# A fused transformer kernel: the third layernorm applied behind the mix, and logits made from the transposed second residual

## The reference, cut to what matters

```python
x = x + relu_attention(layernorm(x), ctx)          # q, k, v with relu, scores over 128 keys
x = x + quantised_ffn(layernorm(x))                # FP6 blocks of 32, one 512x512 weight
# third block: W is 512 x 1024, b has 512
n = layernorm(x)
x = x + n @ W[:, :512].T + (mean(ctx) @ W[:, 512:].T)[:, None, :] + b
# fourth block
n = layernorm(x)
logits = n @ Wg + bg                               # 16 experts
probs = softmax(logits, axis=-2)                   # over the 2048 rows of a batch
vals, idx = top_k(probs transposed, 128)           # 128 rows for each expert
h = relu(n[idx] @ w1 + b1); h = relu(h @ w2 + b2); h = h @ w3 + b3
x = x.at[idx].add(h * vals)
```

## Time and profile before

| what | value |
|---|---|
| runs (3) | 833.03, 833.72, 834.87 us; median 833.72 |
| profiled execution, its own time | 834.25 us |
| its span | 832.4 us, mean granted clock 0.953 |
| PE busy | 727.7 us (87%) |
| DVE busy | 591.7 us (71%) |
| POOL busy | 451.6 us (54%) |
| ACT busy | 412.1 us (50%) |
| DMA | 103.53 MB, 53787 packets |

### The profile page before, as it was taken

How to read it: one execution, slowest core, us unless ns; L and a number is a source line. 1 busy time by engine, 2 the same in 40 slices (tenths; PEclk the granted TensorE clock), 3 DMA queues, 4 the chain that set the end, 5 groups by cost and what they waited for, 6 DMA issues and landing times.

```text
span 832.4 us, 12007 instructions
## 1 busy us (share of the span) xinstructions
PE 727.7 (87%) x4202; PEld 623.9 (75%) x4202; DVE 591.7 (71%) x1010; ACT 412.1 (50%) x564; POOL 451.6 (54%) x627
## 2 busy tenths in 40 slices
PE   1967899999999999999999400899999999999994
PEld 1755788787878878787777300799999999999993
DVE  4685789798897979778695498466666766666751
ACT  4553445555554646445333220366666566666540
POOL 3537788788787878768675060314333344333231
PEclk9979899999999999999999855899999999999998
DMA  9600022121221212111111314448887787887642
GB/s 299 237 0 14 25 76 77 53 89 64 84 70 68 74 53 89 66 39 52 39 65 53 122 69 158 128 134 238 233 244 236 211 251 236 236 240 246 179 88 37
DMA packets 53787, 103.53 MB, mean 124 GB/s; under 512 B 5216, under 2 KB 5984, under 8 KB 53728
## 3 DMA queue, kind: packets, MB, share of 16 engines
q1 hardware_dynamic: 46560, 85.99, 30.9%
q0 software_dynamic: 7168, 16.78, 8.9%
HBM read 77.20 MB, written 25.17 MB: 123 GB/s over the span
## 4 chain that ended last, share of the span: by engine, by line
PE 80%; DVE 10%; POOL 3%; DMA 2%; issue 2%; ACT 2%; SPq 0%; ACTq 0%; POOLq 0%; DVEq 0%
PE bank L238 70%; PE bank L245 8%; DVE pack L1151 1%; PE bank L444 1%; DVE left L1158 1%; DVE pos L1153 1%; DMA x<-x 1%; ACT xn L700 1%; DVE bn L936 1%; POOL rstd L1308 0%; PE bank L555 0%; POOL rstd L1307 0%; DVE x L1088 0%; DMA tok<-xn,ids 0%; DVE s L981 0%
## 5 line engine op out<-in xcount | busy, mean ns | idle before, releaser
L1406 POOL DMA_INDIRECT out<-y,ids x32 | 76.2, 2382 | 173.8 <-DVE y L1271 169.3
L948 DVE TENSOR_TENSOR w_l<-w_raw,w_h 128x2048 fp32r<-128x2048 f32 x45 | 103.0, 2289 | 31.3 <-ACT w_h L704 30.2
L700 ACT ACTIVATE xn<-x,rstd 128x512 f32<-128x512 f32 x96 | 78.6, 819 | 80.0 <-POOL rstd L1312 79.9
L899 ACT ACTIVATE h<-bank,b 128x512 f32<-128x512 f32 x64 | 44.0, 687 | 107.7 <-PE bank L238 107.7
L936 DVE BATCH_NORM_STATS2 bn<-x 128x6 f32<-128x512 f32 x128 | 88.2, 689 | 9.6 <-DMA x<-x 6.3
L704 ACT ACTIVATE w_h<-w_raw 128x2048 fp32r<-128x2048 f32 x48 | 90.6, 1924 | 4.6 <-DMA w_raw<-w 4.6
L948 DVE TENSOR_TENSOR hT_l<-h,hT_h 128x512 fp32r<-128x512 f32 x64 | 44.2, 691 | 67.2 <-ACT hT_h L905 67.2
L245 PE MATMUL bank<-ident,xn 128*128 128x128 f32 x384 | 60.4, 281 | 24.7 <-ACT xn L700 21.4
L245 PEld LDWEIGHTS bank<-ident,xn 128*128 128x128 f32 x384 | 48.5, 145 | 40.6 <-ACT xn L700 28.8
L1308 POOL TENSOR_TENSOR rstd<-rstd,minus_half 128x1 f32<-128x1 f32 x128 | 73.1, 571 | 10.7
L1307 POOL TENSOR_SCALAR rstd<-mean_var 128x1 f32<-128x1 f32 x128 | 31.6, 247 | 82.6 <-DVE mean_var L941 76.0
(11 more groups left out here) (200 smaller groups left out, 2189.5 us busy)
## 6 DMA issues: line engine op xcount, KB each, us to landing
w_raw<-w SPq DMA_DIRECT2D x48, 1024.0 KB, 6.9
x<-x SPq DMA_DIRECT2D x32, 256.0 KB, 2.7
out<-x SPq DMA_DIRECT2D x32, 256.0 KB, 2.0
xn<-xn SPq DMA_DIRECT2D x32, 256.0 KB, 2.0
mask<-mask_t SPq DMA_DIRECT2D x8, 256.0 KB, 3.0
stage<-wc_t SPq DMA_DIRECT2D x2, 1024.0 KB, 8.5
stage<-wq SPq DMA_DIRECT2D x1, 1024.0 KB, 8.2
stage<-wk SPq DMA_DIRECT2D x1, 1024.0 KB, 11.4
```

The source lines that it names most:

```text
L700: act.activation(dst[:, :], src[:, :], ACT.Identity, bias=r[:, n, 2:3], scale=r[:, n, 1:2])\
L899: act.activation(h32[n % 2][:, :], ps_hid[n % 4][:, :], ACT.Relu, bias=bias)
L948: dve.tensor_tensor(dst, src, hi_part, ALU.subtract).then_inc(sem, 1)
L1406: pool.indirect_dma_start(out=out_rows, out_offset=bass.IndirectOffsetOnAxis(ap=ids[:, r:r + 1], axis=0), in_=y[e % 2][b][:, :], in_offset ...
```

## The change

The third layernorm is no longer applied to `x2` before it is transposed. With r = 1/sqrt(var + eps) and m the mean of a row of `x2`, the product is `((x2 - m) r) @ Wc = r (x2 @ Wc')`, where Wc' is Wc with the mean of each of its columns taken off. So `x2` itself is transposed (`x2T_h`, `x2T_l`), and `x3 = r (x2 @ Wc') + x2 + bias` is one operation of VectorE. `xn3` and its ScalarE operation are gone, and `rstd_of(2)` has two operations.

The logits are linear in `x3` up to the fourth layernorm's own factor r4, so they are made from `x2T` with weights of the setup: for each row `x2 @ Wg'` (Wg' is Wg with its column means off) and `x2 @ Gm`, with Gm the mean-free product of Wc' and Wg'. `seg = r4 (x2 @ Wg' + c + r3 (x2 @ Gm)) + bg`. `xn4` is no longer transposed: `t4`, `x4T_h` and `x4T_l` are gone. `logits(g)` is now 8 matmuls, four with 64 columns of weights over the high part and four with 32 over the rest, and stands one step earlier (5, 9, ..., 33). The four 16-row parts go to `seg4` by four DMAs; r3 and r4 of every tile are stored as rows in DRAM, loaded broadcast over partitions after phase 1, and VectorE combines all in six operations ahead of top-k.

New products of the setup, all in plain float32: `mix_means` (4 matmuls with 512 columns of rows moved) and `gate_means` (4 with 16) before `t1(8)`; `mix_gate` (16 with 16) at the end of step 0, from W in its natural layout, loaded once more over 1 MB; `mix_gate_means` (4 with 16) at the end of step 1; `bias_gate` (4 with 2) at the end of step 2. The six warming matmuls of step 34 are gone, and so are the nine that stood there for `t4`.

```diff
     def logits_of(k):
-        g = (k - 6) // GRP
-        return g if (k - 6) % GRP == 0 and 0 <= g < G else None
+        g = (k - 5) // GRP
+        return g if (k - 5) % GRP == 0 and 0 <= g < G else None
...
@sync, after the setup's loads
+        sp.wait_ge(sm.a_set, A["wc1"])
+        sp.wait_ge(sm.g_set, GS["wc1"])
+        sp.dma_start(stage[0][:, :, :], chunked(io.wc[:, 0:D])).then_inc(sm.c_wcn, 16)
+        sp.wait_ge(sm.d_set, V["all"])
+        sp.dma_start(io.cb.rearrange("(a b) n -> a b n", a=1), cbias[0:1, :, :]).then_inc(sm.c_cg, 16)
+        sp.wait_ge(sm.c_cg, 16)
+        for b in range(B):
+            sp.dma_start(cbcol[:, b, :], io.cb[b].rearrange("(c p) -> p c", p=P),
+                         allow_slow_non_contiguous=True).then_inc(sm.c_cg, 16)
...
@sync, after phase 1
+        for i in (1, 0):
+            for b in range(B):
+                rows = io.r[i].rearrange("(b a s t) -> b a s t", b=B, a=1, t=GT)[b].to_broadcast([E, GB, GT])
+                sp.dma_start(rseg[i][64 * b:64 * b + 64, :], rows).then_inc(sem_rseg[i], 16)
...
@tensor
-        def t4(j):
...
         def t3(j):
-            pe.wait_ge(sm.a_xn3, j + 1)
...
+            pe.wait_ge(sm.d_x2, j + 1)
...
-            four_transposes(pe, ps_ta, xn3).then_inc(sm.p_t3, 1)
+            four_transposes(pe, ps_ta, x2[j % 2]).then_inc(sm.p_t3, 1)
...
         def logits(g):
...
+            pe.matmul(ps_s[0:4 * E, :], wgs[:, 0, :], x2_h[:, 0, :], start=True, stop=False)
+            for d in range(C):
+                pe.matmul(ps_s[0:2 * E, :], wgs[:, d, 0:2 * E], x2_l[:, d, :], start=False, stop=False)
+            for d in range(1, C):
+                last = pe.matmul(ps_s[0:4 * E, :], wgs[:, d, :], x2_h[:, d, :], start=False, stop=(d == C - 1))
...
+        def column_means(bank, parts):
+            for d in range(C):
+                last = pe.matmul(bank, mean_w[:, :], parts(d), start=(d == 0), stop=(d == C - 1))
...
+        def mix_gate():
+            pe.wait_ge(sm.c_wcn, 16)
+            pe.wait_ge(sm.a_s, 1)
+            for c in range(C):
+                for o in range(C):
+                    last = pe.matmul(ps_s[:, c * E:(c + 1) * E], stage[0][:, o, c * P:(c + 1) * P], wgf[:, o, 0:E],
+                                     start=(o == 0), stop=(o == C - 1))
...
         q_chunk(*q_of(4))
+        mix_means()
+        gate_means()
         t1(8)
...
-            if valid(k - 3):
-                if not q_units(k):
-                    pe.wait_ge(sm.a_q, N)
-                    keep_warm(4 if valid(k) else 9, wq_h, ps_q[0])
-                t4(k - 3)
+            if valid(k - 3) and k < LAST - 1 and not q_units(k):
+                pe.wait_ge(sm.a_q, N)
+                keep_warm(4 if valid(k) else 9, wq_h, ps_q[0])
...
+            if k == 0:
+                mix_gate()
+            if k == 1:
+                mix_gate_means()
+            if k == 2:
+                bias_gate()
...
@scalar: wc_h now waits for VectorE's subtraction and stands behind norm1(9); in step 2
+            if k == 2:
+                act.wait_ge(sm.p_cb, 3)
+                act.activation(cg[:, :], ps_s[0:E, 128:128 + B], ACT.Copy).then_inc(sm.a_cb, 1)
...
@vector: the subtraction of the column means in the setup, and in phase 1
+            if what == "wc1c":
+                dve.wait_ge(sm.p_set, T["wc1m"])
+                mean = ps_c[:, :].unsqueeze(1).to_broadcast([P, C, D])
+                lo(sm.d_set, stage[0][:, :, :], stage[0][:, :, :], mean)
...
-                dve.tensor_tensor(x3[j % 2][:, :], ps_c[:, :], x2[j % 2][:, :], ALU.add).then_inc(sm.d_x3, 1)
+                dve.scalar_tensor_tensor(x3[j % 2][:, :], ps_c[:, :], r_all[0][:, j:j + 1], x2[j % 2][:, :],
+                                         ALU.mult, ALU.add).then_inc(sm.d_x3, 1)
...
+            if k == 0:
+                dve.wait_ge(sm.p_cb, 1)
+                dve.tensor_copy(wgf[:, :, E:2 * E], ps_s[:, 0:C * E].rearrange("p (c e) -> p c e", c=C))\
+                    .then_inc(sm.d_wg, 1)
+            if k == 1:
+                dve.wait_ge(sm.p_cb, 2)
+                mean = ps_s[:, 0:E].unsqueeze(1).to_broadcast([P, C, E])
+                lo(sm.d_wg, wgf[:, :, E:2 * E], wgf[:, :, E:2 * E], mean)
...
@gpsimd: wc_l stands behind the rest of the queries of unit 4; its subtraction waits for wc_h as before
```

More of the change, by code:

```diff
@@ L102, in build @@
     bk = place("bk", [P, C])
-    bg = place("bg", [E, 1])
+    bg_seg = place("bg_seg", [P, 1])
+    c_seg = place("c_seg", [P, 1])
+    cg = place("logit_shift", [E, B])
+    cbcol = place("mix_bias_col", [P, B, C])
+    r_all = [place(f"rstd_all{i}", [P, N]) for i in range(2)]
     eps_exp = place("minus_half", [P, 1])
@@ L140, in build @@
     at_lt = top[0]
[L141 removed]
+    lt = place("lt", [4 * E, GT])
     q8 = place("q8", [P, D], FP8)
@@ L527, in keys, with mix_gate_means, bias_gate @@
+        def mix_gate_means():
+            pe.wait_ge(sm.d_wg, 1)
+            column_means(ps_s[:, 0:E], lambda d: wgf[:, d, E:2 * E]).then_inc(sm.p_cb, 1)
+        def bias_gate():
+            pe.wait_ge(sm.c_cg, 16 * (1 + B))
+            pe.wait_ge(sm.d_wg, 2)
+            for c in range(C):
+                last = pe.matmul(ps_s[0:E, 128:128 + B], wgf[:, c, 0:E], cbcol[:, :, c], start=(c == 0), stop=(c == C - 1))
+            last.then_inc(sm.p_cb, 1)
         def keys():
```

188 lines of the change are left out of this document (114 added, 74 removed).

## The result

| | before | changed |
|---|---|---|
| runs of this comparison | 833.03 to 834.97 us, median 834.3 (4) | 844.78 to 847.26 us, median 846.07 (4) |
| ratio | 1 | 1.0143, 95% interval 1.0118 to 1.0167 |
| profiled execution, its span | 834.25, 832.4 us | 847.26, 845.4 us |
| PE, DVE, POOL, ACT busy | 727.7, 591.7, 451.6, 412.1 us | 717.3, 585.3, 449.8, 372.1 us |
| DMA packets | 53787 | 65997 |

The kernel is slower by 1.4%. The forecast of 832.9 us, and its whole range up to 840, are missed. Every engine is busy for less time than before, as the prediction worked out, and the time went up all the same. So most of the loss lies in waiting.

The account below looks back on a forecast made before the run. TensorE's instruction sum was taken to bound steps 4 to 26, a loop through several engines steps 28 to 31, then VectorE's top-k. +15.9 - 15.7 - 1.6 + 0.7 and 0.1 less for `wg` made -0.8, so 832.9 us; range 827 to 840.

Parts of the forecast that it names:

- Removed from TensorE: Steps 4 to 26: dropping `t4` and a third of the logits' matmuls shortens TensorE's bound stretch by 15.7 us.
- GpSimd keeps up: Steps 4 to 26: GpSimd needs 10.1 us a step against TensorE's 10.27, tight, so it does not become the bound.
- Steps 28 to 31: Loop through several engines: the step with logits falls from 11.20 to 9.83 us, two others by 0.13 each; -1.6 us.
- Added to the start: Setup and first steps, counted to `t2(3)`: the new products, loads and waits cost +15.9 us.
- (c): Start: SP, held by `wc_l` and loads, brings tile 10 at 94.3, so `ffn(0)` starts at 96.2 instead of 83.76, +12.4 us.
- My lower end: Start: the lower bound of 2.7 us for tile 10's landing, with 7.9 as upper bound and 4.9 taken.
- (b): Start: GpSimd's `wc_l` begins at 77.7, the first rstd after it is 5.2 us later, `t2(0)` at 86.4, `mix_gate` until 92.4.
- The rival with four times a transposition's cost: Start: the small float32 products cost 0.44 us each at full clock, `mix_gate` lasts 7.0 us, total 836.7 us; chance 0.21.
- a load by single elements: Start: `mix_bias_col` is 1024 one-element descriptors, unpriced, speaking for the upper side of tile 10's 2.7 to 7.9 us.
- (d): Steps 1 and 2: half clock, new products and the wait for `bias_gate` before `xdT_h` put `t2(3)` at 130.8.
- The tail: From `t2(31)` to top-k's first maximum: 31.6 us instead of 30.9, the shorter logits' chain spent on a serial step; +0.7 us.
- it lands after 1.9 us: Tail: the last of four logits' pieces, issued at 23.1 us after `t2(31)`, lands 1.9 us later, at 25.0.

Follow-up runs that it names:

- e7: Changed kernel with `mix_gate` and `bias_gate` moved into step 1, the means into step 2, their waits off the path of `xdT_h` and `xdT_l`: 843.87 us.
- e5: Changed kernel with GpSimd writing `x2 + bias` into x3's buffer, so it waits for an earlier store of x3 instead of `t3`: 846.92 us.
- e2: Changed kernel without the 8 row stores of tiles 28 to 31, broadcast loads reading x instead (logits' scaling wrong): 837.95 us.
- e3: Changed kernel with the logits' pieces issued ahead of x3, its normalisation and the rstd row of the same step: 847.53 us.
- e10: Changed kernel with the 64 row stores issued from ScalarE's queue instead of SP's: 846.48 us.
- e9: Changed kernel with only the load of tile 10 moved, ahead of the third load into stage: 845.79 us.
- e1: Changed kernel without its 64 row stores, broadcast loads reading values of x instead (logits' scaling wrong): 836.28 us.
- e6: Changed kernel without row stores or broadcast loads; ScalarE repeats the rstd columns, TensorE transposes them into PSUM, VectorE multiplies by those: 835.36 us.
- e12: Changed kernel with one row store a tile instead of two, both pairs of broadcast loads reading it (logits' scaling wrong): 842.41 us.

## Why the prediction was wrong

Its steps one by one, without their working:

- **Removed from TensorE** (-15.7): right in kind, 2.9 us too much. A group of four steps takes 45.95 us. Missing are 1.4 us in step 3 to 4, where `attend(4)` waits for `s_l`, which e7 shows to be a late effect of the start (it vanishes there), and some 0.3 us in each step behind the scores. "GpSimd keeps up" held otherwise: e5 changed nothing there.
- **Steps 28 to 31** (-1.6): measured +0.8. `attend(28)` waits 2.3 us for `s_l`, and `x2 + bias` waits for `t3`. e5 shows that the second, which the forecast had left out, is worth 1.2 us: without it the step behind the logits takes 9.89 us, and 9.83 was forecast. The first (1.44 us before the change) was not tried apart.
- **Added to the start** (+15.9): +14.2, near, and partly by luck. `t2(0)` moved by 2.9, not 5.2 (in e2, e3 and e10, with the same setup, by 4.5 to 5.0), and from `t2(0)` to `t2(3)`, where I had 44.4, it takes 45.1 here but 42.7 to 43.4 in the traces in which the clock comes back early. The step that failed is (c): tile 10 was there 5 us earlier than I had it, landing 2.8 us after an issue that came 3 us sooner. My lower end was right, and the elementwise loads in front of it were not felt. What came last was `mix_gate`, in (b) taken at 3.65 and measured at 6.84. The rival with four times a transposition's cost said 7.0, but that number was luck: it had 0.44 us for each at full clock. At full clock each takes 3.64 / 16 = 0.23 in e7, and the four of `mix_gate_means` 0.96 together. It is half clock that makes it 0.43, and I had priced half clock at 0.23. e9 shows that tile 10 did not matter, e7 that `mix_gate` and the waits around it were 3.2 us of the start with the clock alike (5.3 against this trace). The waits that (d) named for `ffn(2)` were there: 3.87 us.
- **The tail** (+0.7): measured +11.2. This is what decides the outcome. x3 at `t2(31)` + 16.8 and `xn4` at + 20.7 are as forecast, and so is the issue of the last piece. The step that failed is "it lands after 1.9 us", and the row store in front of it at the price of an issue. The last piece landed after 11.4 us, and the row store, for which the broadcast loads wait too, after 13.0, only 0.6 us before the piece. I took the 1.9 from `seg_logits` of the kernel before, which had no row stores in front of it, and counted the row store itself as one issue on SP and nothing more. In the start I had named a load by single elements as a danger; the 64 stores of the same kind stood in the part of the change that I called cheap, and had neither a bound nor a rival. e1 gives 9.8 us of the 11.2 back, e6, which also takes the loads of rstd away, 10.7 us of the time.

The Trainium skill (DMA: Bandwidth & Descriptors, Specifications) asks for at least 512 B a transfer if the full rate is to be reached, and says that below it the engine does read-modify-write. A store of 4 bytes per descriptor falls under it, and in e1, e6 and e12 the time goes with the number of such stores. No run shows whether it is the read-modify-write or the mere number of packets that costs.

The sum came near zero by two large terms of opposite sign, each known to some 2 to 3 us. Without the row stores (e6) the change comes out at 835.36 us, 2.5 above the forecast and within its range: the frame of the sum held, and a term was left out of it.

## What to carry to other kernels

Price a new small DMA not by its bytes or by its issue, but by its descriptors. Ask who waits for its landing, and then what else is in flight: the duration of a neighbour read from a trace without it is no longer valid. A transfer that is slow all along costs nothing while it has a step to hide in (e1 and e2: 273.2 and 273.4 us in the long stretch), and its full latency where the last one stands on the path; put the test at the end of the loop. A value per row that has to change its layout was cheaper turned on TensorE, which idled there anyway, than written to DRAM column by column (10.7 us). A product placed early in a pipeline that is just filling cost more than its own time here: it ran at half clock, and the in-order engines that picked it up put it in front of the critical operand; one step later the same product took half as long. And before a difference of 2 us between two traces is put down to an edit, compare the granted clock of the stretch in both.
